# An attention and expert layer on one core: the opening of the program is sent in another order

## The reference

```python
# x: (32, 512, 256); 16 heads of 16 channels
qk = x @ W_attn + b_attn ;  q, k = halves of qk ;  v = x (by heads)
y  = causal_attn(q, k, v)                      # softmax(q k' / 4) v
e  = v[1:] - y[:-1] ;  k2 = x[:-1] @ W_k2 + b_k2 ;  q2 = q[1:]
y2 = causal_attn(q2, k2, e), a zero row ahead
x  = layernorm(x + proj(y) + proj(y2))         # proj: W_proj, b_proj
# ffn: 8 experts (swiglu), for the routed rows
x  = layernorm(x + ffn(x))
```

## Time and profile before

| | us |
|---|---|
| median of 3 runs | 2544.13 |
| lowest, highest | 2540.0, 2548.04 |
| the profiled execution | 2552.98 |
| its span | 2551.2 |

### The profile page before, as it was taken

The page is one execution under the profiler, slowest core; times in us unless marked ns, Lnnn a source line. Parts: engine busy times, 40 slices in busy tenths (PEclk is TensorE's granted clock), DMA queues, the critical chain, the costliest instruction groups (busy, mean ns, idle before and its releaser), DMA issues.

```text
span 2551.2 us, 65289 instructions
## 1 busy us (share of the span) xinstructions
PE 2431.7 (95%) x19670; PEld 1277.8 (50%) x19670; DVE 2128.1 (83%) x9397; ACT 1758.5 (69%) x3388; POOL 1507.4 (59%) x2342
## 2 busy tenths in 40 slices
PE   2999999999999999999999999999999999999997
PEld 1555555555555555555455555454555555455454
DVE  2888888888988888889888888888888888888655
ACT  0377777677777777777777777776777777677652
POOL 2366665666666656666666566666656666566432
PEclk8699999999999999999999999999999999999998
DMA  5555555565555555655555566554555655455211
GB/s 96 92 106 91 97 95 102 102 119 106 108 98 100 99 99 105 119 106 107 92 94 107 97 113 118 107 98 89 99 98 107 119 106 106 88 96 101 51 55 54
DMA packets 187783, 251.24 MB, mean 98 GB/s; under 512 B 26768, under 2 KB 103192, under 8 KB 187416
## 3 DMA queue, kind: packets, MB, share of 16 engines
q1 hardware_dynamic: 187440, 247.07, 52.1%
HBM read 74.60 MB, written 16.78 MB: 36 GB/s over the span
## 4 chain that ended last, share of the span: by engine, by line
PE 71%; DVE 13%; issue 7%; DMA 3%; POOL 2%; SPq 2%; ACT 1%; DVEq 0%; ACTq 0%; POOLq 0%
PE score_t L643 22%; PE out_t L604 20%; PE misc L710 9%; DVE junk L845 8%; PE score L654 7%; PE misc L746 5%; PE turn L686 4%; DMA resid<-L_attn_x 2%; PE score L794 2%; SPq L351 1%; DVE max_cols L845 1%; PE misc L733 1%; DVE stats L276 1%; PE score L810 1%; DVE resid L896 1%
## 5 line engine op out<-in xcount | busy, mean ns | idle before, releaser
L845 DVE CUSTOM_DVE_ANT_0 junk<-score,mask_rows 128x384 bf16<-128x384 f32 (+3 forms) x3584 | 1685.9, 515 | 310.8 <-PE score L654 307.6
L513 ACT ACTIVATE prob<-score_t 128x512 f32<-128x512 f32 x2560 | 1399.8, 599 | 576.3 <-PE score_t L643 574.1
L424 POOL TENSOR_SCALAR_AFFINE_SELECT prob<-prob 128x512 f32<-128x512 f32 (+1 forms) x1280 | 711.2, 559 | 832.4 <-ACT prob L513 829.4
L643 PE MATMUL score_t<-stack_q,stack_k 50*128 50x128 f32 (+5 forms) x4096 | 1074.1, 367 | 36.5 <-ACT prob L513 17.5
L654 PE MATMUL score<-stack_k,stack_q 48*128 48x512 f32 (+3 forms) x4096 | 1063.5, 355 | 14.1 <-DMA stack_q<-part_l 12.0
L643 PEld LDWEIGHTS score_t<-stack_q,stack_k 50*128 50x128 f32 (+1 forms) x4096 | 609.0, 185 | 652.8 <-ACT prob L513 539.5
L604 PE MATMUL out_t<-prob,value 128*17 128x512 f32 (+3 forms) x8192 | 719.9, 438 | 12.9 <-POOL prob L424 12.9
L654 PEld LDWEIGHTS score<-stack_k,stack_q 48*128 48x128 f32 x4096 | 616.0, 188 | 26.8 <-DVE max_cols L845 12.6
L845 DVE DVE_READ_ACCUMULATOR2_ANT max_cols<- 128x1 f32 x4096 | 338.5, 83 | 0.0
L604 PEld LDWEIGHTS out_t<-prob,value 128*17 128x17 f32 x8192 | 166.7, 96 | 334.2 <-issue 203.8
L446 POOL TENSOR_TENSOR part_l<-part_f,part_h 128x512 fp32r<-128x512 f32 x192 | 245.9, 1281 | 16.3
(11 more groups left out here) (98 smaller groups left out, 1714.7 us busy)
## 6 DMA issues: line engine op xcount, KB each, us to landing
stack_k<-part_h SPq DMA_DIRECT2D x512, 128.0 KB, 4.2
stack_k<-part_l SPq DMA_DIRECT2D x256, 128.0 KB, 4.5
stack_q<-part_h SPq DMA_DIRECT2D x256, 128.0 KB, 4.2
x_full<-x_turned SPq DMA_DIRECT2D x32, 512.0 KB, 10.8
x_in<-L_attn_x SPq DMA_DIRECT2D x32, 512.0 KB, 14.2
stack_q<-part_l SPq DMA_DIRECT2D x128, 128.0 KB, 5.1
resid<-L_attn_x SPq DMA_DIRECT2D x32, 512.0 KB, 7.8
layer_out<-resid SPq DMA_DIRECT2D x31, 512.0 KB, 5.3
```

The source lines that it names most:

```text
L424: e.affine_select(out=view, in_=view, compare_op=ALU.is_ge, fill=0.0, base=-unit_parts(unit)[1], pattern=[[0, runs], [0, cut], [1, P]], ch ...
L513: e.activation(prob[pair % RING][:, slot % 2 * 512:slot % 2 * 512 + 512], score_t[time % KEY_DEPTH][:, :], ACT.Exp, scale=1.0 / np.sqrt(HE ...
L643: done = e.matmul(score_t[now % KEY_DEPTH][:, col:col + n], keys[rows, pair, kb * P:(kb + 1) * P], stack_q[b % 2][rows, pair, kb * P:token ...
L845: e.tensor_tensor_reduce(junk[count % JUNK][:, 0:n], score[number % MAX_DEPTH][:, col:col + n], mask, 1.0, -3e38, ALU.add, ALU.max, max_co ...
```

## The change

The diff changes the opening in six ways:

- `s_weights` becomes `s_wq` (W_attn and the biases of q and k), `s_wk2` and `s_wproj` (W_proj, b_proj). VectorE and TensorE wait for what they need next; VectorE's doubling of b_proj moves into the loop, beside its copy of x_in.
- The constant rows: `ones` (4 x 4096) becomes `rows_k` and `rows_k2` (4 x 512 each). The two buffers of `stack_k` become one tensor with both behind each other, and so do those of `stack_k2`. Four transfers, each of 4 rows, write both buffers, reading each source row of 512 numbers 16 times over.
- These four are sent behind the first piece's transfers, when they were sent ahead of it. x_in, W_proj and b_proj are sent behind the third piece's.
- x_full of the second batch is sent three units later.
- Each stack transfer waits for its own part (high, then low), for all batches (`stack_piece`), the high ones first.
- The query pieces of batch 0 are sent by ScalarE.

```diff
@@ tensors
-        stack_k = [sb(f"stack_k{i}", [P, pairs, tokens], F32R) for i in range(2)]
-        stack_k2 = [sb(f"stack_k2{i}", [P, pairs, tokens], F32R) for i in range(2)]
+        both_k = sb("stack_k", [P, 2, pairs * tokens], F32R)
+        both_k2 = sb("stack_k2", [P, 2, pairs * tokens], F32R)
+        stack_k, stack_k2 = ([both[:, i, :].rearrange("p (h t) -> p h t", t=tokens) for i in range(2)] for both in (both_k, both_k2))
-        ones = nc.alloc_sbuf_tensor_at("ones", [2 * MAX_PARTS, pairs, tokens], F32R, offset=prob_at)
+        rows_k, rows_k2 = (nc.alloc_sbuf_tensor_at(f"rows_{n}", [2 * MAX_PARTS, tokens], F32, offset=prob_at + 4 * tokens * i)
+                           for i, n in enumerate(("k", "k2")))
@@ new function
+        def stack_piece(e, kind, hf, b, n):
+            stack = {"q": stack_q, "k": stack_k, "k2": stack_k2}[kind][b % 2]
+            terms = PARTS_Q if kind == "q" else PARTS_K
+            for part, tile in enumerate((part_h[n % 2], part_l[n % 2])):
+                e.wait_ge(s_split, 2 * n + part + 1)
+                for term in range(TERMS):
+                    if terms[term] == part:
+                        for side in range(SIDES):
+                            row = SIDE * side + term * HEAD_DIM
+                            e.dma_start(stack[row:row + HEAD_DIM, hf * pairs_half:(hf + 1) * pairs_half, :].bitcast(F32),
+                                        tile[SIDE * side:SIDE * (side + 1), :].bitcast(F32)).then_inc(s_stack[kind, hf], 16)
@@ sync
-            e.dma_start(wq_full ...).then_inc(s_weights, 16)
-            e.dma_start(bias_qk[:, :], b_qk).then_inc(s_weights, 16)
-            e.dma_start(wk2_full ...).then_inc(s_weights, 16)
-            R, M = SCORE_ROWS, MAX_PARTS
-            e.wait_ge(s_ones, 2)
-            for side in range(SIDES):
-                for i in range(2):
-                    e.dma_start(stack_k[i][SIDE * side + R:SIDE * side + R + M, :, :].bitcast(F32), ones[0:M, :, :].bitcast(F32)).then_inc(s_rows, 16)
...
-            e.dma_start(x_in ...).then_inc(s_x, 16)
-            e.dma_start(wp ...).then_inc(s_weights, 16)
-            e.dma_start(bias2 ...).then_inc(s_weights, 16)
+            e.dma_start(wq_full ...).then_inc(s_wq, 16)
+            e.dma_start(bias_qk[:, :], b_qk).then_inc(s_wq, 16)
+            e.dma_start(wk2_full ...).then_inc(s_wk2, 16)
@@ sync, in the loop
-                if (place, slot) == (0, 8) and 1 <= b < batches:
+                if (place, slot) == (3 if b == 1 else 0, 8) and 1 <= b < batches:
...
-                if piece:
+                if piece and not (piece[0] == "q" and piece[2] == 0):
...
+                    stack_piece(e, kind, hf, b, n)
+                    if n == 0:
+                        e.wait_ge(s_ones, 4)
+                        for side in range(SIDES):
+                            first = SIDE * side + SCORE_ROWS
+                            for both, rows in ((both_k, rows_k), (both_k2, rows_k2)):
+                                to = both[first:first + 2 * MAX_PARTS, :, :].rearrange("r i (h t) -> r (i h) t", t=tokens).bitcast(F32)
+                                e.dma_start(to, bass.AP(rows[:, :].tensor, rows[:, :].offset,
+                                                        [list(rows[:, :].ap[0]), [0, 2 * pairs], [1, tokens]])).then_inc(s_rows, 16)
+                    if n == PIECES[1, 9][2]:
+                        e.dma_start(x_in ...).then_inc(s_x, 16)
+                        e.dma_start(wp ...).then_inc(s_wproj, 16)
+                        e.dma_start(bias2 ...).then_inc(s_wproj, 16)
@@ scalar, in the loop, behind the bias addition
+                ended = time - 5
+                piece = piece_ending(ended // SLOTS % UNITS, ended % SLOTS, ended // SLOTS // UNITS, batches)
+                if piece and piece[0] == "q" and piece[2] == 0:
+                    stack_piece(e, *piece)
@@ tensor
-                                e.wait_ge(s_rows, 12 * 16)
+                                e.wait_ge(s_rows, 4 * 16)
...
-                                e.wait_ge(s_weights, WEIGHTS)
+                                e.wait_ge(s_wq, 32)
+                                e.wait_ge(s_wsplit, 2)
+                            if kind == "k2" and b == 0:
                                 e.wait_ge(s_wsplit, 4)
@@ vector
-            e.wait_ge(s_const, 11)
-            e.memset(mask_first[0:1, 0:1], 0.0)
-            e.wait_ge(s_weights, WEIGHTS)
             for i, (parts, full) in enumerate(((wq, wq_full), (wk2, wk2_full))):
+                if i == 0:
+                    e.wait_ge(s_wq, 32)
+                else:
+                    e.wait_ge(s_wk2, 16)
...
-            e.tensor_tensor(bias2[:, :], bias2[:, :], bias2[:, :], ALU.add).then_inc(s_bias, 1)
+            e.wait_ge(s_const, 11)
+            e.memset(mask_first[0:1, 0:1], 0.0)
@@ vector, in the loop, at (5, 2)
+                    if b == 0:
+                        e.wait_ge(s_wproj, 32)
+                        e.tensor_tensor(bias2[:, :], bias2[:, :], bias2[:, :], ALU.add).then_inc(s_bias, 1)
```

More of the change, by code:

```diff
@@ L141, in build_layer @@
         turn = ps("turn", 512)
-        s_weights, s_rows, s_next, s_resid, s_out = (sem(f"s_{n}") for n in ("weights", "rows", "next", "resid", "out"))
+        s_wq, s_wk2, s_wproj, s_rows, s_next, s_resid, s_out = (
+            sem(f"s_{n}") for n in ("wq", "wk2", "wproj", "rows", "next", "resid", "out"))
         s_x, s_xt = sem("s_x"), sem("s_xt")
@@ L290, in _ @@
             e.dma_start(x_full[:, :, :], x_turned[0].rearrange("(h p) t -> p h t", p=P)).then_inc(s_xt, 16)
[L291 to L304 removed]
+            e.dma_start(wq_full[:, :, :, :], w_attn.rearrange("(h p) (w n) -> p h w n", p=P, n=P)).then_inc(s_wq, 16)
+            e.dma_start(bias_qk[:, :], b_qk).then_inc(s_wq, 16)
+            e.dma_start(wk2_full[:, :, :, :], w_k2.rearrange("(h p) (w n) -> p h w n", p=P, n=P)).then_inc(s_wk2, 16)
             for time in times:
@@ L347, in _ @@
                         e.wait_ge(s_key, SLOTS * (reader + 1))
-                    for term, part in enumerate(PARTS_Q if kind == "q" else PARTS_K):
+                    stack_piece(e, kind, hf, b, n)
+                    if n == 0:
+                        e.wait_ge(s_ones, 4)
                         for side in range(SIDES):
-                            row = SIDE * side + term * HEAD_DIM
-                            e.dma_start(stack[row:row + HEAD_DIM, hf * pairs_half:(hf + 1) * pairs_half, :].bitcast(F32),
-                                        parts[part][SIDE * side:SIDE * (side + 1), :].bitcast(F32)).then_inc(s_stack[kind, hf], 16)
+                            first = SIDE * side + SCORE_ROWS
[4 more added lines that the diff above has]
+                    if n == PIECES[1, 9][2]:
+                        e.dma_start(x_in[:, :, :], x[0].rearrange("(t p) c -> p t c", p=P)).then_inc(s_x, 16)
+                        e.dma_start(wp[:, :, :], w_proj.rearrange("(h p) n -> p h n", p=P)).then_inc(s_wproj, 16)
+                        e.dma_start(bias2[:, :], b_proj.rearrange("(o n) -> o n", o=1).to_broadcast([P, width])).then_inc(s_wproj, 16)
                 for a, b in ((0, ahead + 1), (1, ahead)):
```

14 lines of the change are left out of this document (5 added, 9 removed).

## The result

The changed kernel is slower: 2577.78 us (median of 4 runs, 2570.72 to 2581.65) against 2546.09 (4 runs, 2540.0 to 2549.99) for the kernel before, a ratio of 1.0124 with a 95% interval of [1.0093, 1.0155]. The forecast was 2529 (2517 to 2538), with 0.83 for faster. The profiled execution took 2576.76 us.

A forecast was written before the change was run, and what follows sets the result against it. It took TensorE's opening waits as the bound, chiefly 33.1 us for the weight split. The third group would start 15.0 us earlier after a new 8.3 us stall: 2544.1 - 15.0 = 2529 us, range 2517 to 2538.

The forecast's parts named there:

- the last sentence on the other queues: Steady state: the same transfers go 1.3 us earlier and nobody waits for them, at worst 1 us in all.
- The "slower" rival: Opening: constant rows pass at half of 27 GB/s, 39 us, second keys land at 80.9, 2554 us; chance 0.06.
- First matmul at 11.0: Opening: TensorE's first matmul at 11.0 us (10.0 to 12.0), after the x split, against 33.05.
- the bound of 1.9: Opening: most that VectorE's casts and subtractions beside GpSimd's could delay the x split, 1.9 us; 1.0 taken.
- First keys at 15.3, queries at 17.8: Opening: first key transfer leaves at 15.3 us, and ScalarE sends the first queries at 17.8.
- The rows sit on four engines: Opening: each four-row constant transfer occupies four of 16 DMA engines, 64 packets of 2 KB on each, none elsewhere.
- The price: Opening, constant rows: 0.30 us a packet where the four engines have nothing else, 0.15 where alternating with other queue's packets.
- First score at 32.0: Opening: first score matmul at 32.0 us (30.4 to 33.9), 23.2 earlier, waiting for the first queries.
- ScalarE's sends are hidden: Opening: ScalarE's 12 new query sends, 0.6 us each between bias additions, cost nothing.
- A second stall of 8.3 us, third group at 56.0: Opening: third attention group waits 8.3 us for second keys behind the rows, starts at 56.0 in place of 70.96.
- x_in and b_proj hidden: Opening: x_in, W_proj and b_proj behind the second keys just hidden, up to 3 us if SyncE's sends are held back.
- the prediction's row: Opening: trace row of DMA shares, from which a send's bytes reach the DMA engines 1.4 us after it.

The follow-up runs named there:

- m_before_parts: Kernel before, with only the later pieces' sends changed (each stack transfer waits for its own part, high ones first, from the second batch on): 2597.43 us, ratio 1.0174.
- l_rows_spread: Changed kernel, constant rows sent per buffer when due, later pieces sent as before, resid and x_full slots exchanged, x_next's last 127 rows cut in two: 2499.84 us, ratio 0.9817.
- o_q_sync: l_rows_spread with the first batch's query pieces sent by SyncE again in place of ScalarE: 2498.3 us, ratio 0.9798.
- c_later_old: Changed kernel with batches from 1 on sent as before (waits for both parts, order high, low, high), opening as changed: 2539.95 us, ratio 0.9945.
- g_split: Changed kernel with x_next's last 127 rows sent as 112 rows and 15 rows: 2515.95 us, ratio 0.9882.
- a: Changed kernel with key pieces of batches from 1 on in the old order (high, low, high), part-wise waits kept: 2555.7 us, ratio 1.0015.
- b: Changed kernel with transfers of batches from 1 on waiting for both parts, high ones still first: 2541.48 us, ratio 0.9940.
- n_before_split: Kernel before with only x_next's last 127 rows sent as 112 and 15: 2523.86 us, ratio 0.9891.

## Why the prediction was wrong

**The step that failed** is the last sentence on the other queues: "In the steady state the same transfers go 1.3 us earlier and nobody waits for them: nothing, at worst 1 us in all." The steady state lost 37.0 us in the profile, and m_before_parts measures the changed sends alone at 1.74%, 44 us. That nobody waits for the stack transfers was true; what is queued behind them was left out. resid had been waited for in 19 of 26 batches before the change (34.9 us), so it had no slack, and the transfer stood on that kernel's own page, with 2% of the chain of work that ended last. I had read the profile's waits only up to 60 us for this part, because I had located the change in the opening, though its diff altered every batch. The row that told of the one-engine piece was among those I cited the earlier trace rows, and so was x_in's landing of 11.9 us behind a transfer on few engines; I used both for the opening only. The "slower" rival had a mechanism of the opening (0.06) and none of the loop.

**The opening, step by step.**
- *First matmul at 11.0:* 11.32. VectorE's 1.23 us subtraction took 2.17 beside GpSimd, and GpSimd's subtraction took 1.58 for 1.26 and the cast behind it 1.60 for 0.61; its chain ended 1.4 us late (11.17 for 9.78), within the bound of 1.9. The Trainium skill's rule of an exclusive port pair (SBUF — State Buffer, "Who interferes with whom") is borne out as far as both engines slowed together; whether one at a time was fully blocked, the durations don't tell, since both lengthened.
- *First keys at 15.3, queries at 17.8:* 15.64 and 18.10. Right.
- *The rows sit on four engines:* right in kind (share 0.25), and moving the rows moved the clog. The price was right too: in the last two stretches above four engines move 27 to 29 GB/s, which is 0.28 to 0.30 us a packet (2 KB by a quarter of the rate). In the stretches with 33 GB/s and more, faster packets of keys and queries (some 85 ns each in the trace) are among them.
- *First score at 32.0:* 42.76, and 47.7 to 48.1 in five others. Wrong by 11 to 16 us. I let the two queues alternate packet for packet on the four engines. In the trace, some 2.5 transfers of queries (10 packets an engine by my count) lasted 13 us longer than in a free queue: each seems to have waited for a whole transfer of rows, 16 packets an engine, before its own four, and 2.5 x 16 x 0.30 us is 12. That it alternates by transfers is argued from these durations, not shown by a run of its own. The Trainium skill (DMA: Bandwidth & Descriptors, "Queues, rings and completion order") says that an engine drains about 9 to 17 descriptors of one queue before it turns to the next; the trace agrees with that grain better than with mine.
- *ScalarE's sends are hidden:* they took 7.32 us for two and held back the third piece's bias addition to 28.39. While the rows are in flight, a send holds the engine that sends. With the rows out of the way the same two take 1.44 us (l_rows_spread), and o_q_sync shows that ScalarE's sending then costs nothing.
- *A second stall of 8.3 us, third group at 56.0:* 0.93 us, third group at 59.49. The late first score had absorbed it. So 11.5 us were gained where 15.0 were forecast; c_later_old's opening gained 7.4.
- *x_in and b_proj hidden:* right; VectorE's copy of x_in starts at 62.49, 3.0 us behind the third group, and waits for nothing.

Had the steady state cost nothing, as assumed, c_later_old says what would have come: 0.9945 [0.9926, 0.9964] of the kernel before, 9 to 19 us gained. That holds the 15 forecast, though at the first masked score the profiles show only half of it (7.4), and the steady state of c's profile was no faster than before's (73.70 for 73.46). That c meets the forecast is therefore in part luck: the opening's stalls were other than forecast, and no row shows where the rest of c's gain is.

**How the early sends reach resid.** The packets in the kept traces show it. resid is 512 packets of 1 KB, 32 for each of 16 engines. In the kernels below 480 of them have started by 5 to 6 us after its send. With the one-engine piece in place the last 32 then come one behind the other, which is the share of one engine at its 24 GB/s (1 KB in 43 ns). Medians over the batches between 400 and 2300 of the profiles:

| kernel | resid sent, us after the one-engine piece | the 32 begin, after that piece | time between two of them, ns | last one begins, after resid's send |
|---|---|---|---|---|
| before | 18.95 | 24.2 | 43 | 6.5 |
| c_later_old | 19.1 | 24.2 | 43 | 6.4 |
| after | 17.6 | 23.7 | 118 | 9.1 |
| m_before_parts | 17.6 | 23.8 | 117 | 9.4 |
| g_split | 17.1 | 22.1 | 4 | 5.4 |

So one engine is behind the fifteen others, and gets to resid some 24 us after the piece, though resid is sent 1.3 us sooner behind it after the change. That it is the piece's engine follows from g_split, where the packets of all engines end together (4 ns apart). The next keys are sent 24.2 us after the piece before and 22.9 after, and their first bytes move 1.4 us later by the prediction's row: before, at 25.6, when the 32 packets have gone by (24.2 and 32 x 43 ns make 25.6); after, at 24.3, in the middle of them, and the packets are then 118 ns apart for 43. That it is the keys' packets which stretch the tail is argued from these times.

**Left open.** No run moved those keys alone. Why a's part of the early sends costs less than the keys' other two is not shown either (its last packet begins at 8.1). What runs show is that the loss needs both the early sends (b) and the one-engine piece (g_split).

## What to carry to other kernels

An edit in a helper that every batch calls is a change of every batch: look up in the steady state which transfer is waited for already, and ask what each send that moves will stand in front of, for all that is queued behind it. Count for each transfer how many DMA engines it occupies: one of 127 rows in 72 us cost this kernel 1.1% (n_before_split), and cutting it in two is worth more than the changed opening. When an early send makes a kernel slower, look for the queue it joins too soon.

## What the runs showed that was not expected

- One transfer of 127 KB on one engine lengthened x_in's landing from 4.7 to 14.1 us and its send from 0.39 to 2.86, though fifteen engines were free of it.
- Sends are not free behind transfers on few engines: on SyncE 13.68 us for four that otherwise take 2.6, on ScalarE 7.32 for two that otherwise take 1.4.
- A piece of 5.3 us on one engine is still felt 24 us later: that engine comes last to resid's packets.
- Four neighbouring rows moved no faster than two: 27 to 29 GB/s after, 27 before.
- The same opening differed by 5 us between executions (first score 42.76 against 47.7 to 48.1), which is as much as many an opening edit is worth.
